# Attention scores from two rounded 32-bit parts on two row tiles, in an attention and mixture-of-experts layer on one core

## The reference, cut to what matters

```python
x = L0_attn_x                                   # (2, 2048, 256), float32
def attn(x):                                    # 16 heads of 16, D = 256, DL = 64
    q, k, v = x @ W_q, x @ W_k, x @ W_v
    latent = (k + v) @ W_down_kv
    k_rec = heads(latent @ W_up_k); v_rec = heads(latent @ W_up_v); qh = heads(q)
    scores = einsum('bhqd,bhkd->bhqk', qh, k_rec) / sqrt(256)
    scores = scores * exp(-0.01 * abs(t_q - t_k))
    return merge(softmax(scores) @ v_rec) @ W_o
x = x + layernorm(attn(layernorm(x)))
x = x + layernorm(ffn(layernorm(x)))            # 2 shared experts, 16 routed, top 2
```

## Time and profile before

| | |
|---|---|
| median of 3 runs | 1757.76 us (1753.49 to 1758.03) |
| profiled execution | 1757.73 us, its span 1756.0 us |
| first score starts | 117.96 us |
| attention (first exp of head 0 to the last) | about 119 to 1225 us |
| feed-forward stage | to the end |
| busy in the span | PE 94%, ACT 66%, DVE 35%, POOL 3% |
| 16 DMA engines | 20.2% of the span, 104 MB |

### The profile page before, as it was taken

The page is one execution under the profiler, slowest core; times in us unless marked ns, Lnnn a source line. Parts: engine busy times, 40 slices in busy tenths (PEclk is TensorE's granted clock), DMA queues, the critical chain, the costliest instruction groups (busy, mean ns, idle before and its releaser), DMA issues. The chain is left out here.

```text
span 1756.0 us, 26320 instructions
## 1 busy us (share of the span) xinstructions
PE 1650.1 (94%) x8752; PEld 646.0 (37%) x8753; DVE 613.8 (35%) x1688; ACT 1163.8 (66%) x1330; POOL 59.9 (3%) x104
## 2 busy tenths in 40 slices
PE   7639999999999999999999999998899999999996
PEld 5502222222222222222222222223465565466454
DVE  5804324234143242341341111112344434534432
ACT  4428898988998987989988999998232232222210
POOL 1000000000000000000000000000000000000000
PEclk9969999999999999999999999999899999999998
DMA  7412122122222221222222111123110000100000
GB/s 193 120 64 72 64 76 78 62 75 74 72 74 65 77 73 59 73 79 72 73 62 81 50 44 58 55 87 78 31 37 24 32 16 24 36 12 24 13 12 14
DMA packets 104017, 104.68 MB, mean 60 GB/s; under 512 B 46576, under 2 KB 91376, under 8 KB 103712
## 3 DMA queue, kind: packets, MB, share of 16 engines
q1 hardware_dynamic: 103968, 104.08, 20.2%
HBM read 70.51 MB, written 33.55 MB: 59 GB/s over the span
## 5 line engine op out<-in xcount | busy, mean ns | idle before, releaser
L683 ACT ACTIVATE work<-ps 128x1024 f32<-128x1024 f32 x1024 | 993.9, 1025 | 139.7 <-DVE ps L511 73.4
L604 PE MATMUL ps<-stack 96*128 96x512 bf16 (+3 forms) x2432 | 552.3, 350 | 56.0 <-POOL work L475 32.1
L613 PE MATMUL ps<-work 128*32 128x512 f32 x4096 | 550.6, 610 | 0.0
L511 DVE TENSOR_TENSOR ps<-ps,small 128x128 f32<-128x128 f32 x512 | 153.1, 299 | 804.9 <-PE ps L604 804.9
L604 PEld LDWEIGHTS ps<-stack 96*128 96x128 bf16 x2432 | 189.4, 98 | 620.8 <-ACT work L683 252.2
L1568 PE MATMUL ps<-xT,stack 128*128 (+1 forms) x320 | 156.4, 612 | 1.5 <-PEq L430 1.5
L613 PEld LDWEIGHTS ps<-work 128*32 128x32 f32 x4096 | 81.3, 108 | 189.1 <-ACT work L683 112.0
L1576 PE MATMUL ps<-xT,stack 128*128 (+1 forms) x320 | 150.4, 592 | 0.0
L1591 PE MATMUL ps<-stack,work 128*128 128x256 f32 x640 | 141.3, 380 | 0.0
L1541 ACT ACTIVATE work<-ps 128x512 f32<-128x512 f32 x80 | 47.6, 595 | 135.5 <-PE ps L1568 135.3
L1591 PEld LDWEIGHTS ps<-stack,work 128*128 128x128 f32 x640 | 120.6, 190 | 15.8 <-issue 0.2
(11 more groups left out here) (119 smaller groups left out, 806.9 us busy)
## 6 DMA issues: line engine op xcount, KB each, us to landing
parts_dram<-part SPq DMA_DIRECT2D x64, 384.0 KB, 4.0
stack<-parts_dram SPq DMA_DIRECT2D x128, 192.0 KB
stack<-parts_dram SPq DMA_DIRECT2D x128, 128.0 KB
work<-in_L_attn_x SPq DMA_DIRECT2D x16, 512.0 KB, 5.0
stack<-parts_dram SPq DMA_DIRECT2D x128, 64.0 KB
attn_dram<-work SPq DMA_DIRECT2D x16, 256.0 KB, 14.0
work<-attn_dram SPq DMA_DIRECT2D x8, 512.0 KB, 3.9
out<-work SPq DMA_DIRECT2D x8, 512.0 KB, 3.0
```

The lines of the kernel that those rows point to most:

```text
L511: nc.vector.tensor_tensor(own_block(s), own_block(s), dmask, ALU.mult).then_inc(s_["masked"], 1)
L604: m = nc.tensor.matmul(ps[:, half_of(s, half) + q0 // CH % 2, q0 % CH:q0 % CH + w], stack[0:ROWS, par, k, s * P:(s + 1) * P], stack[0:ROWS ...
L613: m = nc.tensor.matmul(ps[STRIP * c:STRIP * (c + 1), ACC + par], Vg[:, par, s], probs[:, probs_of(par, s), chunk(c)], start=s == 0, stop=s ...
L683: nc.scalar.activation(probs[:, probs_of(par, s), half * HALF:(half + 1) * HALF], src, ACT.Exp, scale=SCALE).then_inc(s_["exp_done"], 1)
```

## The change

The operands are split into two parts instead of three, both rounded to the type float32r and kept in 4 bytes. All four products of parts are taken: 4 x 16 = 64 rows. The keys are held twice, on partitions 0 to 63 and 64 to 127 (`K_st`); the queries of half 0 lie on the upper 64 partitions and those of half 1 on the lower 64 (`Q_st`). `scores(par, n, s)` now issues the pieces of both halves, alternating between the two row tiles, ahead of `products`, and waits once, with the count that half 1 needs. `load_halves` uses 16 transfers for a head, each with at least 16 rows outside, 3 MB in all where it was 1.5 MB; the copies to DRAM are 8 bytes a number where they were 6. In attention each prepare has three pieces instead of five, in steps 8 to 10 and 12 to 14 of the even head. Before the first load SP also waits for the last normalisation, since `Q_st` lies where the prologue keeps its blocks. A separate copy of the old prologue (`prologue_shifted`) serves the version that is not taken.

```diff
+TILE_ROWS = 4 * HD
+HALVES_DMAS = 16
...
+        K_st = nc.alloc_sbuf_tensor_at("K_st", [P, 2, 2, S], F32R, offset=stack_at)
+        Q_st = nc.alloc_sbuf_tensor_at("Q_st", [P, 2, 2, S // 2], F32R, offset=work_at + 4 * 3 * S)
...
+def store_halves(sp, halves_dram, part, rows, c, which, done):
+    cols = chunk_at(c)
+    for a in range(2):
+        dst = halves_dram[2 * which + a].rearrange("h d i s -> (h d) i s")[rows, :, cols]
+        sp.dma_start(dst, part[:, which, a]).then_inc(done, 16)
+
+
+def load_halves(sp, K_st, Q_st, halves_dram, m, par, done):
+
+    for a in range(2):
+        keys = halves_dram[2 + a].rearrange("h d i s -> (h d) i s")[bass.ds(m * HD, HD)]
+        queries = halves_dram[a].rearrange("h d i s -> (h d i) s")[bass.ds(m * 2 * HD, 2 * HD)]
+        for g in range(2):
+            for i in range(2):
+                at = g * TILE_ROWS + 2 * HD * i
+                src = keys[:, i:i + 1, :].to_broadcast([HD, 2, S])
+                sp.dma_start(K_st[at:at + 2 * HD, par, a, :].bitcast(F32), src).then_inc(done, 16)
+                src = queries[:, g * (S // 2):(g + 1) * (S // 2)]
+                sp.dma_start(Q_st[at:at + 2 * HD, par, a, :].bitcast(F32), src).then_inc(done, 16)
...
-            load_stack(sp, stack, parts_dram, 0, 0, stack_in)
+            sp.wait_ge(xn_ready, NB)
+            load_halves(sp, K_st, Q_st, halves_dram, 0, 0, stack_in)
...
-                nc.vector.tensor_copy(pt[:, :, 0], split).then_inc(prep_link, 1)
-                dve.wait_ge(prep_link, 3 * k + 1)
-                nc.vector.tensor_tensor(split, split, pt[:, :, 0], ALU.subtract).then_inc(prep_link, 1)
-                dve.wait_ge(prep_link, 3 * k + 2)
-                nc.vector.tensor_copy(pt[:, :, 1], split).then_inc(prep_link, 1)
-                dve.wait_ge(prep_link, 3 * k + 3)
-                nc.vector.tensor_tensor(pt[:, :, 2], split, pt[:, :, 1], ALU.subtract).then_inc(prep_sb, 1)
+                nc.vector.tensor_copy(pt[:, :, 0].bitcast(F32R), split).then_inc(prep_link, 1)
+                dve.wait_ge(prep_link, k + 1)
+                nc.vector.tensor_tensor(pt[:, :, 1].bitcast(F32R), split, pt[:, :, 0], ALU.subtract).then_inc(prep_sb, 1)
...
-            def scores(par, n, s, half):
-                wait(pe, "exp_done", halves_done(n, s, half))
-                for q0, w, q, k in score_pieces(s, half):
-                    m = nc.tensor.matmul(ps[:, half_of(s, half) + q0 // CH % 2, q0 % CH:q0 % CH + w],
-                                         stack[0:ROWS, par, k, s * P:(s + 1) * P],
-                                         stack[0:ROWS, par, q, q0:q0 + w], start=True, stop=True)
-                m.then_inc(s_["sc_ps"], 1)
+            def scores(par, n, s):
+
+                wait(pe, "exp_done", halves_done(n, s, 1))
+                halves = [list(score_pieces(s, half)) for half in range(2)]
+
+                late = len(halves[0]) > len(halves[1])
+                order = [(0, 0), (1, 0), (0, 1), (0, 2), (1, 1)] if late else [(half, i) for i in range(3) for half in range(2)]
+                for half, i in order:
+                    if i < len(halves[half]):
+                        q0, w, a = halves[half][i]
+                        tile = slice(half * TILE_ROWS, (half + 1) * TILE_ROWS)
+                        m = nc.tensor.matmul(ps[:, half_of(s, half) + q0 // CH % 2, q0 % CH:q0 % CH + w],
+                                             K_st[tile, par, a, s * P:(s + 1) * P], Q_st[tile, par, a, q0 % HALF:q0 % HALF + w],
+                                             start=True, stop=True)
+                        if i == len(halves[half]) - 1:
+                            m.then_inc(s_["sc_ps"], 1)
...
                     for s in range(NSTEP):
-                        scores(par, n, s, 0)
+                        scores(par, n, s)
                         if s >= 2:
                             products(par, n, s - 2)
                         elif not (first and par == 0):
                             products(1 - par, n - 1, NSTEP - 2 + s)
-                        scores(par, n, s, 1)
```

More of the change, by code:

```diff
@@ L9 @@
 BF16 = mybir.dt.bfloat16
+F32R = mybir.dt.float32r
 ALU = mybir.AluOpType
@@ L39, with aligned @@
 FLAGS = 936
+def aligned(at):
+    return (at + 31) // 32 * 32
 def emit(nc, io):
@@ L57, in emit @@
         w_unit = sb("w_unit", [P, 2, KD, P])
+        stack_at = aligned(nc.sbuf_base)
         stack = sb("stack", [P, 2, 4, S], BF16)
         part = sb("part", [P, 2, 2, 3, CH], BF16)
+        work_at = aligned(nc.sbuf_base)
         work = sb("work", [P, 17408])
+        K_st = nc.alloc_sbuf_tensor_at("K_st", [P, 2, 2, S], F32R, offset=stack_at)
+        Q_st = nc.alloc_sbuf_tensor_at("Q_st", [P, 2, 2, S // 2], F32R, offset=work_at + 4 * 3 * S)
         ps = ctx.enter_context(nc.psum_tensor("ps", [P, 8, CH], F32))
@@ L64, in emit @@
         attn_dram = dram("attn_dram", [T, D])
+        halves_dram = nc.dram_tensor("halves_dram", [4, B * H, HD, 2, S], F32, kind="Internal").ap()
         parts_dram = nc.dram_tensor("parts_dram", [4, 3, B * H, HD, S], BF16, kind="Internal").ap()
@@ L68, in emit @@
                       w_qk=w_qk, w_unit=w_unit, stack=stack, part=part, work=work, ps=ps,
-                      attn_dram=attn_dram, parts_dram=parts_dram)
-        prologue(**common, shifted=False)
+                      attn_dram=attn_dram, parts_dram=parts_dram, halves_dram=halves_dram, K_st=K_st, Q_st=Q_st)
+        prologue(**common)
         layer(**common, attend=attention)
@@ L79, in emit @@
             common["sem"] = lambda n: nc.alloc_semaphore("s_" + n)
-            prologue(**common, shifted=True)
+            prologue_shifted(**common)
             layer(**common, attend=attention_shifted)
@@ L117, in load_stack @@
             sp.dma_start(stack[row * HD:(row + count) * HD, par, kind, :], parts).then_inc(done, 16)
-def prologue(nc, io, sem, ident, xT, V_all, decay, small, w_qk, w_unit, stack, part, work, ps, parts_dram, shifted, **_):
+def store_halves(sp, halves_dram, part, rows, c, which, done):
[14 more added lines that the diff above has]
+                sp.dma_start(Q_st[at:at + 2 * HD, par, a, :].bitcast(F32), src).then_inc(done, 16)
@@ L122, in prologue, with prologue_shifted @@
+def prologue_shifted(nc, io, sem, ident, xT, V_all, decay, small, w_qk, w_unit, stack, part, work, ps, parts_dram, **_):
     w_k = carve(work, 0, KD, D)
@@ L201, in _ @@
                     nc.gpsimd.tensor_copy(w_unit[:, :, :, :], w_qk[:, :, :, 0:P]).then_inc(w_set, 1)
-                if shifted and n >= NB - 4:
+                if n >= NB - 4:
                     if n == NB - 4:
```

783 lines of the change are left out of this document (486 added, 297 removed).

## The result

The changed kernel takes 1770.64 us, the median of four runs (1769.08 to 1771.64), against 1757.89 for the kernel before: ratio 1.0075, 95% interval 1.0054 to 1.0096. It is **slower by 0.75%**, where 1728 us was forecast; the interval leaves 1 out, so the sign is certain, though the size is under 2%. Its profiled execution took 1770.11 us, its span 1768.3.

The account below looks back on a forecast made before the run. TensorE was taken to bound attention, leading ScalarE by only 7%, while the prologue waited on transfers. From 1757.7 us, 24 less in the prologue and 6 less in attention gave 1728 us, range 1708 to 1752.

Parts of the forecast that it names:

- The prologue: Before attention: shorter prepares and faster loads start the first score at 94.4 instead of 117.96, 24 us less (14 to 28).
- One cycle a column: Score matmuls in attention: rounded 32-bit operands stream one column a cycle, as bf16 does, about 385 ns for 512 columns.
- two-cycle rival: Score matmuls in attention take two cycles a column, so the kernel is slower at 1928 us; chance 0.17.
- Tiles at the same time: Attention scores: both halves' row tiles run together; the rival that they don't gave 1831 us, chance 0.09.
- S = 0.64: Attention: a half's scores come 0.64 us after the group's start, 0.60 plus 0.04 for 4-byte load and interleaving.
- its two savings: Whole kernel: 24 us less in the prologue and 6 us less in attention.
- loads that don't hide: Attention scores: each tile's second 4-byte weight load costs 0.11 us, giving 1765 us; chance 0.12.
- The chain argument: Attention steps 1 to 7: exp, scores, mask and hand-overs follow in a chain, 2.09 us a step against 1.97 before.
- Steps 8 to 15: Attention: the mask lies beside half 0's exp, so a step takes 1.83 us, ScalarE's own pace.
- Boundaries: Between heads in attention: 3.0 us from even to odd, 3.7 from odd to even, and 2.74 for the next step.
- Projections: Attention's 12 pairs with projections, at steps 7 and 11: 2.8 us more a pair, 68.9 us.
- The turning point: Attention: the change becomes a loss where the time from a group's start to its half's scores passes 0.75 us.

Follow-up runs that it names:

- e7: Kernel before the change, with its stack loaded in 24 transfers of 16 rows in place of 12; 1731.90 us, ratio 0.9860.
- e2: Kernel before, given two 64-row tiles in bf16 and the changed kernel's order, third parts left out, stack in 32 transfers; 1737.20 us.
- e3: Changed kernel's operands and loads, with the order and waits of the kernel before; 1722.18 us, ratio 0.9815.
- e1: Changed kernel without the diagonal tile's mask, and ScalarE's wait for it, in steps 0 to 7 of a head; 1739.15 us.
- e9: Kernel of e1 with ScalarE's two waits swapped: products' buffer first, scores last; 1717.23 us.
- e10: Changed kernel with the previous head's products ahead of the scores in the first two steps of even heads; 1759.00 us.

## Why the prediction was wrong

The forecast had the mechanism and the places, and missed the sign by two sizes that point the same way.

- **The prologue: right in kind, 20 us for 24.** Rounding to 4 bytes takes 0.69 us, the lower bound, so prepares end at 72.8, within 69 to 73.5. The loads began 1.1 us later than said, and took 17.8 us for 15: 16 issues took 9.9 us, not 11.5, but the last landed some 8 after its issue, not 3.5, with the engines busy 0.86 at 226 GB/s, some 260 at all of them. The 300 GB/s taken from the share of attention was too much. The Trainium skill, "DMA: Bandwidth & Descriptors", "How many engines", lets a transfer use as many engines, up to 16, as divide its outer dimensions; the trace agrees in direction (the engines are busy 0.18 before and 0.86 here, 0.46 in run e7).
- **One cycle a column: right.** Records of 512 columns take 385 to 393 ns; with that the two-cycle rival falls. **Tiles at the same time: right**, the second starts 3 ns after the first, and four pieces take 0.73 us; that rival falls too.
- **S = 0.64: the step that failed.** The mechanism was right and this term too small: it measured 0.73. The 0.04 "for the 4-byte load ahead" was an estimate between 0 and 0.11; run e2 shows 0.12 (0.73 against 0.61). By the forecast's own price of 13 us for 0.05, that is 23 of the 41 us by which the forecast missed its two savings; with it the forecast would have been 1751. Run e2 says the same from the other end: with S at 0.61, and less the 11.8 us by which its first exp comes later than the changed kernel's, it takes about 1725 us. The choice between 0 and 0.11 went by the earlier trace rows, eight matmuls of one kind in a row, each load beside the matmul ahead of it. Here every group follows work that is tiled in another way. In the kernel before, the scores' 2-byte load starts 107 and 426 ns ahead of its matmul behind transposes and projections, which are not tiled, as the scores then were, and 4 ns ahead behind the products' column tiles. In the changed kernel, where the scores lie in row tiles, the 4-byte load starts 2 ns ahead behind all three. The rows spoke neither way: the transposes' spacing of 0.11 is a load's length, but also that of 128 columns at two cycles.
- **The rival "loads that don't hide" came out within 6 us**: forecast pairs of 68.3 and 71.3, measured 68.1 and 71.3; total 1765, and 1769 with the prologue's 4. Its reason was not right, so the hit is in part luck. It put the 0.11 on each tile's second load. The second matmul starts 0.34 us behind the first, its load beside it; the first load is the bare one. The Trainium skill, "TensorE: Matmul & The Clock Gate", Part 3, says that a load overlaps running matmuls only where the row group differs. That would have the second ones bare, on the same rows; the trace doesn't agree, with the 0.34 us above.
- **The chain argument: right.** 1.02 + 0.05 + 0.73 + 0.04 + 0.30 + 0.03 = 2.17, measured 2.18 to 2.31 in masked steps. Where a group has five pieces or follows transposes, 0.05 to 0.13 come on top, which the forecast put at 0.1 a head. Steps 8 to 15: 1.84 for 1.83. Boundaries: 3.09 for 3.0 and 3.79 for 3.7; the second step of an even head 2.92 for 2.74. Over a quiet pair 68.1 for 66.1, of which the 14 masked steps, transposes included, are 1.7.
- **Projections: 3.2 a pair for 2.8.** The forecast's own terms, 3.43 less 2.09 and 3.43 less 1.83, make 2.9; the group in them is 0.66 and not 0.55, twice, which is most of the rest. In all: 12 x 2.4 + 4 x 2.0 = 37 us on the attention's side, 4 on the prologue's; -30 + 41 = +11, measured +12.
- **The turning point was named too high.** "A loss where S passes 0.75" left out the prologue's 4 us and what came on top of S; by the forecast's own 13 us for 0.05, the measured +12 at 0.73 puts it near 0.68. With an estimate of 0.64 between bounds of 0.60 and 0.71, a chance of 0.12 for the upper end was too small.

What stays open: what makes the load go ahead of its matmul behind some work and not behind other, why the last of 16 transfers lands 8 us after its issue when attention's land in a median of 5.7, and what exactly keeps a step with five pieces 0.05 longer.

## What to carry to other kernels

Before making the engine that bounds a loop cheaper by regrouping its work, write down the longest chain that the new grouping closes and compare it with the second engine's pace: here TensorE's step fell from 1.97 to 1.66 us, the group then waited for one exp more, and order and wait cost some 50 us (run e3). Price the weight load at every place where a group of matmuls follows work that is tiled in another way, whether the engine idled there or not: here 0.11 us more in 4 bytes than in 2, once a group, and next to nothing for the pieces that follow in the same tiles. And when such a regrouping disappoints, look at the order of what hangs on it (which half carries the mask, what stands first at a boundary, which buffer comes next) before giving it up: the same operands gave 1770.6 us in one order and 1660.6 in another.

## What the runs showed of the hardware

- A rounded 32-bit matmul streams one column a cycle (385 to 393 ns for 512 columns), and two row tiles of 64 rows start 3 ns apart and run at the same time: four pieces in 0.73 us. They also overlap, in part, where they are neighbours in the queue by chance (run e3, four pieces in 0.90 us).
- Two row tiles with 4-byte weights of 128 columns take 0.11 us more for the first matmul of a group than with 2-byte ones (496 against 387 ns; the load's record 183 against 93). It is so after idle time (the changed kernel) and without it (run e3, 407 groups behind products). The tile's next load, beside the running matmul, adds next to nothing (385 to 394 ns, against 376 with 2-byte operands).
- In the kernel before a 2-byte load starts 107 and 426 ns ahead of its matmul behind transposes and projections, and 4 ns ahead behind products in column tiles.
- On ScalarE a wait that sits on a register instruction ahead of the exp made it start 0.116 us after the event, a wait on the exp itself 0.036 (runs e1 and e9: 22 exps in 21.14 and 20.39 us).
- After 3.1 us in which TensorE was busy 1.23, the granted clock was 0.50 for 3.4 us, and eight product records took 1.93 us in place of 1.06 (run e10); it came at ten places between the first and the last head of that kernel, and at none there in the changed kernel.
